# Layer 0's side sums in bf16 parts, and attention's one-hots earlier, in a four-layer graph network

## What is computed

```python
h = (x @ W).reshape(n, H, C)
a_src = (h * att_src).sum(-1); a_dst = (h * att_dst).sum(-1)
alpha = leaky(a_src[src] + a_dst[dst])
m = segment_max(alpha, dst)
ex = exp(alpha - m[dst])
denom = segment_sum(ex, dst)
out = segment_sum(h[src] * (ex / denom[dst])[..., None], dst) + bias
```

## Time and profile before

| | us |
|---|---|
| median of 3 runs | 5755.3 (5745.56 to 5755.92) |
| the profiled execution | 5750.34 |
| its span | 5748.5 |
| attention, from the first broadcast row to the last pick | 97 to 690 |
| maxima and the exponential | 690 to 809.6 |
| layer 0's sums | 809.6 to 1541 |
| norms, then layer 1 | 1541 to 2769.5 |
| layers 2 and 3 | 2769.5 to 5748.5 |

### The profile page before, as it was taken

One profiled execution on the slowest core, in us unless ns is written; L12 is line 12 of the kernel. 1 busy time (PEld: TensorE's weight loads), 2 busy tenths in 40 slices (PEclk: granted clock), 3 DMA queues, 4 the chain that ended last, 5 costly groups with the idle time before them and its releaser, 6 DMA issues.

```text
span 5748.5 us, 124694 instructions
## 1 busy us (share of the span) xinstructions
PE 4340.3 (76%) x26535; PEld 3551.3 (62%) x26536; DVE 3626.2 (63%) x10847; ACT 1734.3 (30%) x5601; POOL 3890.9 (68%) x3352
## 2 busy tenths in 40 slices
PE   3666549999729898989577777777773688888884
PEld 3555549999719888888455555555552455555553
DVE  5666775555665444444655555555554688888886
ACT  0000000000001111111266665666663244445442
POOL 4777787770016777777288888888885477777771
PEclk6555555555555555555699888889886899999997
DMA  5666535552123233223044444444444344445441
GB/s 122 193 188 188 163 105 164 163 164 75 46 75 84 78 77 77 78 76 77 20 35 36 35 35 36 35 35 36 35 36 79 107 135 134 134 134 135 133 134 40
DMA packets 396077, 536.69 MB, mean 93 GB/s; under 512 B 86434, under 2 KB 273900, under 8 KB 396001
## 3 DMA queue, kind: packets, MB, share of 16 engines
q0 software_dynamic: 213152, 301.19, 27.6%
q1 hardware_dynamic: 134897, 125.62, 7.2%
q10 hardware_dynamic: 47952, 109.14, 6.4%
HBM read 408.63 MB, written 127.00 MB: 93 GB/s over the span
## 4 chain that ended last, share of the span: by engine, by line
PE 25%; POOL 19%; issue 17%; DMA 17%; DVE 17%; ACT 3%; SPq 1%; DVEq 1%; ACTq 1%; POOLq 0%
POOL ACCB L460 12%; DMA acc_dram<-GR,ARENA 12%; PE WIDE L613 9%; POOL acc_dram L469 5%; DMA ARENA<-p_dram,SRCI 4%; PE WIDE L615 3%; DVE ACCB L1002 3%; POOL ARENA L486 2%; DVE ARENA L1184 2%; PE WIDE L724 2%; PE WIDE L549 2%; DVE ARENA L1002 2%; PE WIDE L706 2%; DVE T L1002 2%; DVE ARENA L1522 1%
## 5 line engine op out<-in xcount | busy, mean ns | idle before, releaser
L469 POOL DMA_INDIRECT acc_dram<-GR,ARENA x830 | 1283.2, 1546 | 349.1 <-ACT GR L812 221.7
L452 POOL DMA_INDIRECT GR<-h_dram,SRCI x830 | 911.9, 1099 | 327.4 <-issue 241.6
L486 POOL DMA_INDIRECT ARENA<-p_dram,SRCI x830 | 864.5, 1042 | 302.3 <-issue 154.8
L460 POOL DMA_INDIRECT ACCB<-h_dram,SRCI x830 | 805.1, 970 | 276.6 <-issue 251.7
L724 PEld LDWEIGHTS WIDE<-ACCB 128*128 128x128 f32 x3320 | 544.4, 221 | 390.5 <-issue 283.2
L724 PE MATMUL WIDE<-ACCB 128*128 128x128 f32 x3320 | 597.0, 310 | 234.9 <-issue 234.9
L651 PE MATMUL WIDE<-ACCB 128*128 128x128 f32 x1660 | 648.4, 494 | 122.7 <-DMA ACCB<-h_dram,SRCI 84.4
L1002 DVE TENSOR_TENSOR ACCB<-iota,DLC 128x640 f32<-128x640 f32 x332 | 274.7, 827 | 695.2 <-PE WIDE L653 377.9
L1431 DVE SCALAR_TENSOR_TENSOR ACCB<-WIDE,ARENA,ACCB 128x128 f32<-128x128 f32 x1660 | 567.7, 350 | 181.3 <-ACT ACCB L910 162.5
L613 PE MATMUL WIDE<-ACCB 128*128 128x128 f32 x1660 | 642.9, 491 | 33.6 <-DVE ACCB L1002 33.6
L1006 DVE TENSOR_SCALAR ACCB<-ACCB,SRC 128x128 f32<-128x128 f16 x832 | 291.1, 350 | 480.1 <-ACT ACCB L812 472.0
(11 more groups left out here) (317 smaller groups left out, 8046.5 us busy)
## 6 DMA issues: line engine op xcount, KB each, us to landing
T<-pairs_dram ACTq DMA_DIRECT2D x167, 320.0 KB, 3.8
g_dram<-GR SPq DMA_DIRECT2D x166, 320.0 KB
ACCB<-g_dram ACTq DMA_DIRECT2D x166, 320.0 KB, 3.0
ARENA<-src_rows_dram SPq DMA_DIRECT2D x166, 160.0 KB, 3.0
GR<-h_dram,SRCI POOLq DMA_INDIRECT x830
ACCB<-h_dram,SRCI POOLq DMA_INDIRECT x830, 2.5
acc_dram<-GR,ARENA POOLq DMA_INDIRECT x830
GR<-in_attr SPq DMA_DIRECT2D x830, 16.0 KB
```

The lines of the kernel that those rows point to most:

```text
L452: pool.indirect_dma_start(GR[:, q, :], None, h_dram[:, :], row_of(j)).then_inc(landed[q], 16)
L460: pool.indirect_dma_start(GX[:, q, :], None, h_dram[:, :], row_of(j)).then_inc(l1_landed[q], 16)
L469: pool.indirect_dma_start(acc_dram[q % NACC][:, :], bass.IndirectOffsetOnAxis(ap=SCI[:, j:j + 1], axis=0), GR[:, q, :], None, compute_op=A ...
L486: pool.indirect_dma_start(HC3[:, j % RING3, :], None, p_dram[:, :], bass.IndirectOffsetOnAxis(ap=SRCI[:, j:j + 1], axis=0)).then_inc(lande ...
```

## The change

The nine f32 columns of `EXF` become 26 bf16 columns `EXB` (`EXC`): three bf16 parts each of ex and of the maxima, whose sum is the f32 value, and two columns of ones. They are made before the loop by ACT and DVE in turn. Layer 0's product of line 615 becomes a bf16 product with `OHB`, a bf16 copy of the f32 one-hot that ACT makes for each group (`l0_cast`, behind `l0_load`). The counts that layer 1 made with its column of ones come from the new column, so layer 1's line 653 goes. After the loop DVE adds the three parts. In attention the one-hots get four buffers and run two groups ahead of the pick, and PE's loop is written with `by_groups`, four groups per pass, each reading its own five tile numbers.

```diff
@@ attention, PE @@
-            with pe.Fori(0, ITER) as i:
-                ts = tile_registers(ENG.PE, i)
-                for h in range(2):
-                    n = i * 2 + h + 1
...
+            def a_values(i, g):
+
+                ts = tile_registers(ENG.PE, i, g * GROUP, LRING, GROUP)
+                h, n = g % 2, i * LONG + g + 1
+                pe.wait_ge(ev("a_onehot"), n + ABUFS)
+                pe.wait_ge(ev("a_picked"), n)
+                pe.wait_ge(ev("a_adas_copied"), n)
...
+            by_groups(pe, a_values)
@@ layer 0, PE @@
-                pe.wait_ge(ev("l0_messages"), i * LONG + g + 1)
+                pe.wait_ge(ev("l0_onehot_cast"), i * LONG + g + 1)
+                pe.wait_ge(ev("l0_messages"), i * LONG + g + 2)
...
-                    pe.matmul(EXTP[:, t, :].rearrange("p a b -> p (a b)"), onehot,
-                              EXF[:, bass.ds(i * LRING + q, 1), :].rearrange("p a b -> p (a b)"),
+                    pe.matmul(EXTP[:, t, :].rearrange("p a b -> p (a b)"), OHB[:, h, k, :],
+                              EXB[:, bass.ds(i * LRING + q, 1), :].rearrange("p a b -> p (a b)"),
@@ layer 1, PE @@
-                    counted = pe.matmul(EXTP[:, bass.ds(ts[k], 1), 0:1].rearrange("p a b -> p (a b)"),
-                                        OH01[:, h * HALF + k, :], ones[:, 0:1], start=False, stop=False, skip_group_check=True)
@@ ACT @@
+            act.activation(EXF[:, :, 0:HEADS], EXF[:, :, 0:HEADS], ACT.Exp).then_inc(ev("ex"), 1)
+            act.wait_ge(ev("ex"), 1)
+            copy(EXB[:, :, 0:4], EXF[:, :, 0:HEADS]).then_inc(ev("ex_part"), 1)
+            act.wait_ge(ev("ex_rest"), 1)
+            copy(EXB[:, :, 12:16], REST[0]).then_inc(ev("ex_part"), 1)
+            act.wait_ge(ev("ex_rest"), 2)
+            copy(EXB[:, :, 8:12], REST[1]).then_inc(ev("ex_part"), 1)
+
+            def l0_cast(i, g):
+
+                h = g % 2
+                act.wait_ge(ev("l0_onehot"), i * LONG + g + 1)
+                copy(OHB[:, h, :, :], OH01[:, h * HALF:(h + 1) * HALF, :]).then_inc(ev("l0_onehot_cast"), 1)
@@ attention, DVE @@
-                v.wait_ge(ev("a_picked"), i * ABUFS + b + 1)
-                ts1(OTB[:, h, :], BCAST[:, b, :], pcol[:, 0:1], ALU.is_equal)
+                if not isinstance(i, int) or m >= 2:
+                    v.wait_ge(ev("a_picked"), m - 1)
+                ts1(OTB[:, b, :], BCAST[:, b, :], pcol[:, 0:1], ALU.is_equal)
...
-                    a_onehot(i + (b + 1) // ABUFS, (b + 1) % ABUFS)
+                    a_onehot(i + (b + 2) // ABUFS, (b + 2) % ABUFS)
                     a_pick(i, b)
@@ before layer 0's loop, DVE @@
-            link(v.tensor_copy(EXF[:, :, 8], FIRSTC))
...
-            v.wait_ge(ev("ex"), 1)
+            link(v.tensor_copy(EXB[:, :, 4:8], EXF[:, :, 4:8]))
+            link(tt(REST[0], EXF[:, :, 4:8], EXB[:, :, 4:8], ALU.subtract))
+            v.sem_inc(ev("ex_rest"), 1)
+            link(v.memset(EXB[:, :, 24:EXC], 1.0))
+            v.wait_ge(ev("ex_part"), 1)
+            link(tt(REST[1], EXF[:, :, 0:4], EXB[:, :, 0:4], ALU.subtract))
+            v.sem_inc(ev("ex_rest"), 1)
+            v.wait_ge(ev("ex_part"), 2)
+            link(tt(EXB[:, :, 20:24], REST[0], EXB[:, :, 12:16], ALU.subtract))
+            v.wait_ge(ev("ex_part"), 3)
+            link(tt(EXB[:, :, 16:20], REST[1], EXB[:, :, 8:12], ALU.subtract))
+            v.sem_inc(ev("l0_messages"), 1)
@@ after layer 0's loop, DVE @@
-            link(v.tensor_copy(EXT[:, :, :], EXTP))
+            link(v.tensor_copy(CNT[:, :], EXTP[:, :, 24]))
+            link(v.tensor_copy(EXT[:, :, 0:8], EXTP[:, :, 0:8]))
+            for part in range(1, 3):
+                link(tt(EXT[:, :, 0:8], EXT[:, :, 0:8], EXTP[:, :, 8 * part:8 * part + 8], ALU.add))
```

More of the change, by code:

```diff
@@ L60 @@
 BIG = 1e30
+EXC = 3 * 2 * HEADS + 2
+EXT_AT = 7 * 512 - 14 * EXC
+DEG_AT = EXT_AT + NT * EXC
+assert NT * D <= EXT_AT and DEG_AT + NT <= 8 * 512
 EPS = 1e-5
@@ L122, in gnn_stack @@
         ADAS = carve(ARENA, SPAD * 4, SPAD, 8)
-        EXF = carve(ARENA, SPAD * 12, SPAD, 9)
+        EXF = carve(ARENA, SPAD * 13, SPAD, 2 * HEADS)
+        EXB = carve(ARENA[:, 0:SPAD * EXC // 2].bitcast(BF16), 0, SPAD, EXC)
+        REST = [carve(T12, SPAD * 4 * k, SPAD, HEADS) for k in range(2)]
         DR, SR, TR, DL, HI, LO, VALID, FIRST = [carve(ARENA, SPAD * (12 + k), SG, P) for k in range(8)]
@@ L539, in _ @@
             pe.wait_ge(ev("slots_loaded"), 32)
-            with pe.Fori(0, ITER) as i:
-                ts = tile_registers(ENG.PE, i)
-                for h in range(2):
-                    n = i * 2 + h + 1
[L544 to L555, removed]
+            def a_values(i, g):
[4 more added lines that the diff above has]
+                pe.wait_ge(ev("a_adas_copied"), n)
+                for k in range(HALF):
+                    for part in range(3):
+                        pe.matmul(bank(h)[:, k * NT * HEADS:(k + 1) * NT * HEADS], OTP[:, g, k, 1, :],
+                                  ADNB[:, part, :, HEADS:2 * HEADS], start=(part == 0), stop=(part == 2))
+                    for part in range(3):
+                        last = pe.matmul(bank(2 + h)[:, k * 8:(k + 1) * 8], OTP[:, g, k, 0, :],
+                                         ADNB[:, part, bass.ds(ts[k], 1), :].rearrange("p a b -> p (a b)"),
+                                         start=(part == 0), stop=(part == 2))
+                last.then_inc(ev("a_values"), 1)
+            by_groups(pe, a_values)
             pe.wait_ge(stage_done, STAGE["edge_values"])
@@ L598, in _ @@
             clear_nodes().then_inc(ev("l0_cleared"), 1)
-            pe.matmul(bank(7, NT), identb[:, :], zerob[:, 0:1].broadcast_to([P, NT]), start=True, stop=False, skip_group_check=True
+            pe.matmul(bank(7), identb[:, :], zerob[:, 0:1].broadcast_to([P, 512]), start=True, stop=False, skip_group_check=True
                       ).then_inc(ev("l0_cleared"), 1)
@@ L611, in l0_sum @@
                     t = bass.ds(ts[k], 1)
-                    onehot = OH01[:, h * HALF + k, :]
-                    pe.matmul(NODES[:, t, :].rearrange("p a b -> p (a b)"), onehot, GX[:, q, :],
+                    pe.matmul(NODES[:, t, :].rearrange("p a b -> p (a b)"), OH01[:, h * HALF + k, :], GX[:, q, :],
                               start=False, stop=False, skip_group_check=True)
-                    pe.matmul(EXTP[:, t, :].rearrange("p a b -> p (a b)"), onehot,
-                              EXF[:, bass.ds(i * LRING + q, 1), :].rearrange("p a b -> p (a b)"),
+                    pe.matmul(EXTP[:, t, :].rearrange("p a b -> p (a b)"), OHB[:, h, k, :],
+                              EXB[:, bass.ds(i * LRING + q, 1), :].rearrange("p a b -> p (a b)"),
                               start=False, stop=False, skip_group_check=True)
-                    last = pe.matmul(bank(7, NT), LOA0[:, h, k, :], HIA0[:, h, k, :], start=False, stop=False,
+                    last = pe.matmul(DEGP, LOA0[:, h, k, :], HIA0[:, h, k, :], start=False, stop=False,
                                      skip_group_check=True)
@@ L863, in l0_load @@
                               ).then_inc(ev(f"l0_loaded{g}"), 16)
+                l0_cast(i, g)
             by_groups(act, l0_load)
```

51 lines of the change are left out of this document (26 added, 25 removed).

## The result

The changed kernel takes 5739.5 us (median, 5726.9 to 5748.7) beside 5754.3 us for the kernel before on the same chip: a ratio of 0.9975, 95% interval 0.9968 to 0.9981. It is faster, by some 15 us where the forecast said 73 to 78, and 17 us above the upper end of the range. The profiled execution has a span of 5732.3 us against 5748.5.

A forecast was written before the change was run, and what follows sets the result against it. Bounds: PE's queue in attention, PE's weight loads in layer 0's sums, POOL's gathers in layer 1. Terms +33 + 16 - 120 + 1 - 3 = -73 us from the profiled 5750 gave 5677 us; range 5640 to 5722.

The forecast's parts named there:

- PE is not its limit: Layer 1: POOL's gathers set the pace, so PE's removed weight loads gain little; with ring stall and tail, -3 us.
- Attention, +33: Attention: more reads of tile numbers on PE's queue lengthen the stage by 33 us, bounds +11 and +75.
- The loads with their steps: Attention: four five-number loads in four groups, 4.5 us beside gathers, plus 0.16 us of steps for each of three.
- the loop ends that go: Attention, PE's loop: two loop ends of 0.50 us each become one in four groups.
- The lead: Attention: DVE's one-hots two groups ahead are worth nothing, as DVE never gates PE; zero us.
- Rival (a): Attention: DVE does gate PE, so the one-hots' lead pays, -73 us, and the loads hide; 5571 us, chance 0.05.
- rival (b): Attention: the loads hide behind queued matmuls, +0 there; 5644 us, chance 0.10.
- Before layer 0's sums, +16: Before layer 0's sums: splitting off bf16 parts on ACT and DVE delays the start by 16 us, 12 to 22.
- Layer 0's sums, -120: Layer 0's sums: cheaper L615 weight loads bring 731 us to 611, -120 us, bounds -143 and -47.
- The pace of 3.68: Layer 0's sums: us per group, set by PE's queue of address steps and one load; the array alone 3.55.
- Rival (d): Layer 0's sums: L613's columns already hide L615's weight loads, a group stays at 4.40 us; 5797 us, chance 0.05.
- rival (c): Layer 0's sums: ACT's queue becomes the limit, row load behind the cast; 5813 us at 7 us landing, chance 0.04.

## Why the prediction was wrong

**The step that failed** is layer 1, "PE is not its limit": -3 forecast, +56.9 measured. The sentence is true, and the conclusion from it was not. POOL's gathers set the stage, and PE's speed decided when DVE's one-hots fell among them. I asked of the removed product whose time it takes, and not whose timing. I even named what fails here: before layer 0's sums the gathers "would be held up by DVE's large operations". The longest gather of the earlier trace rows, 8108 ns, shows it in the kernel before; it ends 0.75 us behind the scan that runs on DVE when it starts:

```profile
700.75 8.11 POOL L452 DMA_INDIRECT GR<-h_dram,SRCI  x1 [0.30 <-issue]
...
700.48 7.62 DVE L1212 TENSOR_TENSOR_SCAN ACCB<-T 128x3584 f32<-128x3584 f32 x1
```

For layer 1, with an operation of 0.83 us, I put it at nothing without a reason.

The clue stood in the earlier trace rows too: a longest gather of 1580 ns at a median of 944. 830 x 0.944 are 784 us; the busy time in that stretch was 805. Those 21 us were already holds, and had I asked what made a gather long, a kernel with the one-hots' phase changed would have been a rival on the slower side: at worst all 166 one-hots hold a gather by some 0.5 us, 83 us less the 21 there already, +62, and 5677 + 62 = 5739. With 151 long gathers it came near that worst case. That the sum gives the measured 5739 is chance, as the terms ahead of layer 1 were off by some 8 us.

**Attention, +33:** +30.9, by two sizes that err against each other. The loads with their steps cost 42.7 where the sum had (0.82 + 0.48) x 41.5 = 54; the loop ends that go gave 10.6 where it had 0.50 x 41.5 = 21. The lead is worth 1.2 us: zero was right, and the waits that put PE's idle time on DVE were rightly not believed. Rival (a) falls with it; rival (b) falls by the 42.7.

**Before layer 0's sums, +16:** +15.2.

**Layer 0's sums, -120:** -124.0, and up to 9 more in the other runs that leave this stage as changed. The pace of 3.68 was right as a mean of two: 3.74 beside the gathers, where PE's queue is the limit, and 3.39 after them. The array's own pace was mis-sized: 3.55 forecast, 3.33 measured in the run without loads. Rival (d), hidden weight loads, falls. So does rival (c): PE's pauses in these sums, apart from the first, were put down to issue and none to ACT.

**The gap to the end, 0:** +4.5 us after the last gather. The stretch takes 2982.3, 2986.3 and 2988.3 us in the three runs that edit the kernel before elsewhere, so that is within what executions differ by.

**The chances.** Faster by over 0.2% came in, by 0.25%. The range failed because it was made from the unknown sizes of terms in the sum; the term that failed had one value and no bounds.

## What to carry to other kernels

Work taken off an engine that isn't the limit still moves in time what waits for it; where two engines hold each other up, ask how their instructions will lie against each other, and look at the longest of a kind of instruction beside its median before calling a stage's pace fixed. If 830 equal gathers have a mean above the median, something holds some of them, and shorter instructions on the engine that does it cost less than they seem to. Numbers that a loop reads into registers on the queue of the limiting engine are to be counted like its other instructions. In this kernel fewer, larger reads helped in attention, where that queue alone was the limit, and cost time in layer 0's sums, for a reason that stays open.

## What the runs showed of the hardware

An indirect gather on POOL takes 0.94 us by itself. In layer 1, one that starts while a DVE instruction runs ends 0.81 to 0.83 us after that instruction. This was so with the tensor_tensor of 128x640 in f32 (153 of 153 gathers of the changed kernel, 1.59 us at most), with the scalar_tensor_tensor of 128x128 (115 of 115 that start 0.10 to 0.20 us behind one, in the run with the one-hot 0.3 us later) and with the f32 tensor_scalar of 128x128 (25 of 25 that start 0.09 to 0.15 us behind a piece). So the gather loses what is left of the DVE instruction, less some 0.13 us, and an instruction of 0.3 us costs it almost nothing. A gather that starts almost together with the DVE instruction is not held: 20 within 0.04 us behind the one-hot of the kernel before, 70 within 0.07 us behind the scalar_tensor_tensor in the run named, all at 0.94 to 0.95 us.

The Trainium skill (SBUF — State Buffer, Who interferes with whom) states that a DVE instruction with two SBUF inputs contends with a GpSimd instruction that reads SBUF, that the port pair they share is an exclusive lock, and that the order of issue decides which one blocks. The rows agree where the DVE instruction comes first. Where the gather comes first they show no block: 130 one-hots of the kernel before start beside a running gather and take 0.82 to 0.85 us, and those gathers take their 0.94. The same section puts tensor_tensor among the operations that did not stall a DMA, and gives as an inferred reason that it takes only the read interface; the runs here differ: the gather is stalled.

A read of tile numbers into PE's registers takes 0.58 us (smallest) to 1.23 (median) for five numbers and 1.08 to 2.00 for ten, in attention. In layer 0, while the gathers last, the median for five is 1.38 and the longest 2.40; after them it is 1.24 and the longest 1.26. It isn't the gathers alone, which run in attention too. The Trainium skill (Runtime: NRT & Kernel Launch, Instruction fetch mechanics) gives some 200 ns a register for the loads at a launch, by estimate 1.0 and 2.0 us: here, in a loop, the median for ten agrees, that for five is 0.2 longer, and the smallest of both are near half.
